# Ten products of zeros ahead of a row search, and transform steps issued three at a time, in a two-layer graph attention kernel

## What is computed

```python
xr = jnp.einsum('nd,rdf->rnf', x, W)              # one transform of all nodes per edge type
oi, oj = xr[etype, dst], xr[etype, src]
alpha = jax.nn.leaky_relu(oi @ q + oj @ k, 0.2)
m = segment_max(alpha, dst); e = exp(alpha - m[dst]); z = segment_sum(e, dst)
out = segment_sum((e / (z[dst] + 1e-16))[:, :, None] * oj, dst) + b
# h = elu(layer 1); out = layer 2 of h; result = layernorm(x + out)
```

## Time and profile before

| | |
|---|---|
| median of three executions | 1293.2 us (1292.36 to 1293.78) |
| the profiled execution's own time | 1294.57 us |
| its span, first to last instruction | 1292.6 us |
| PE busy | 1249.7 us, 97% of the span |
| DVE busy | 989.4 us, 77% |
| ACT busy | 757.7 us, 59% |
| mean granted clock of PE | 0.992 |

### The profile page before, as it was taken

How to read it: one execution, slowest core, us unless ns; L and a number is a source line. 1 busy time by engine, 2 the same in 40 slices (tenths; PEclk the granted TensorE clock), 3 DMA queues, 4 the chain that set the end, 5 groups by cost and what they waited for, 6 DMA issues and landing times.

```text
span 1292.6 us, 18743 instructions
## 1 busy us (share of the span) xinstructions
PE 1249.7 (97%) x7104; PEld 1121.7 (87%) x7104; DVE 989.4 (77%) x1289; ACT 757.7 (59%) x1210; POOL 4.9 (0%) x20
## 2 busy tenths in 40 slices
PE   6899999999999999999999999999989999999996
PEld 4766656665699999999999999999989999999995
DVE  4678899999399899999989967759844466656554
ACT  4655432332499889979979942257434444464462
POOL 1000000000000000000000000000000000000000
PEclk9999999999999999999999999999989999999998
DMA  9420131111553333323313237944486776778860
GB/s 314 164 92 31 44 122 49 50 50 43 194 122 103 103 96 103 96 68 116 118 50 99 64 109 236 313 160 159 159 307 235 248 246 204 264 261 305 283 230 34
DMA packets 93847, 195.32 MB, mean 151 GB/s; under 512 B 16125, under 2 KB 66366, under 8 KB 93762
## 3 DMA queue, kind: packets, MB, share of 16 engines
q1 hardware_dynamic: 93568, 193.77, 45.1%
q0 software_dynamic: 96, 0.23, 0.1%
q10 hardware_dynamic: 98, 0.16, 0.0%
HBM read 154.28 MB, written 39.85 MB: 150 GB/s over the span
## 4 chain that ended last, share of the span: by engine, by line
PE 76%; DVE 13%; ACT 4%; DMA 3%; issue 3%; SPq 1%; PEld 1%; ACTq 0%; DVEq 0%
PE ps L1174 24%; PE ps L1132 24%; PE ps L959 13%; PE ps L984 10%; DMA arena<-in_L_gnn_W 3%; DVE arena L1319 3%; PE ps L1036 3%; DVE arena L1376 2%; DVE arena L1380 2%; ACT arena L718 1%; ACT arena L719 1%; DVE ps L1448 1%; DVE misc L1329 1%; DVE arena L1461 1%; DVE arena L1398 1%
## 5 line engine op out<-in xcount | busy, mean ns | idle before, releaser
L1132 PE MATMUL ps<-arena 128*128 128x193 f32 x2400 | 396.9, 327 | 1.8 <-DVE arena L1380 1.5
L1132 PEld LDWEIGHTS ps<-arena 128*128 128x128 f32 x2400 | 392.1, 190 | 4.3 <-DVE arena L1380 3.8
L959 PE MATMUL ps<-arena,xT 128*128 128x384 f32 (+1 forms) x720 | 249.6, 494 | 0.0
L718 ACT ACTIVATE arena<-arena,misc 128x640 f32<-128x640 f32 x240 | 196.9, 820 | 31.5 <-DVE arena L1376 23.7
L959 PEld LDWEIGHTS ps<-arena,xT 128*128 128x128 f32 x720 | 131.4, 191 | 76.4 <-issue 0.3
L719 ACT ACTIVATE arena<-arena,misc 128x640 f32<-128x640 f32 x240 | 195.7, 815 | 0.0
L1376 DVE TENSOR_TENSOR arena<-arena 128x1280 f32<-128x1280 f32 x120 | 178.4, 1486 | 20.9 <-ACT arena L719 20.8
L1380 DVE SCALAR_TENSOR_TENSOR arena<-arena,Ct 128x1280 f32<-128x1280 f32 x120 | 179.2, 1493 | 15.0 <-DVE arena L1376 11.0
L1319 DVE SCALAR_TENSOR_TENSOR arena<-arena,misc 128x1250 f32<-128x1250 bf16 x108 | 155.8, 1520 | 1.5 <-ACT arena L663 1.5
L835 ACT ACTIVATE g_hi<-arena 128x512 fp32r<-128x512 f32 (+2 forms) x90 | 49.7, 552 | 158.8 <-PE ps L1174 143.6
L1174 PE MATMUL ps<-x2a,g_hi 128*128 128x384 f32 (+1 forms) x600 | 131.8, 342 | 5.2 <-issue 5.2
(11 more groups left out here) (174 smaller groups left out, 1356.8 us busy)
## 6 DMA issues: line engine op xcount, KB each, us to landing
x2a<-xr_d SPq DMA_DIRECT2D x45, 776.0 KB, 4.3
x2b<-xr_d SPq DMA_DIRECT2D x45, 776.0 KB, 4.5
arena<-xr_d SPq DMA_DIRECT2D x120, 193.0 KB, 2.4
xr_d<-stg SPq DMA_DIRECT2D x60, 384.0 KB, 3.0
arena<-ab_d SPq DMA_DIRECT2D x12, 1280.0 KB, 6.4
xr_d<-bb SPq DMA_DIRECT2D x60, 193.0 KB, 2.2
arena<-in_L_gnn_W SPq DMA_DIRECT2D x5, 2304.0 KB, 9.8
arena<-in_L_gnn_W SPq DMA_DIRECT2D x7, 1152.0 KB, 6.8
```

The costliest lines, as they stand in the source:

```text
L718: nc.scalar.activation(weights1(g, r, t)[:, h, :], abr[:, r, h, :], ACT.Exp, bias=qk1t[:, t, col + R * H:col + R * H + 1])
L959: last = mm(unit1_bank(u)[:, 0:w], xT[:, kt, t * P:(t + 1) * P], v, start=kt == 0, stop=kt == KT - 1)
L1132: last = mm(bank1(g, i)[:, o:o + HD + 1], weights1(g, r, t)[:, h, i * P:(i + 1) * P], xring[t % NX][:, o:o + HD + 1], start=False, stop=Tr ...
```

## The change

Two edits. First, PE issues NWARM = 10 products of zeros (bf16, 128 by 128 by 512 columns, into `ps[3]`, which nothing has written yet and whose next use starts afresh) after its wait for the constants and ahead of its wait for `ranks`. Second, `steps0` gives BATCH = 3 steps at a time: 20 batches over the same 79 pairs, so behind pairs 30, 34, 38 and so on to 102, and behind pair 105. No step is added or left out; the order among pairs and among steps stays. ACT's count of the units that are still to be taken out after the loop follows the new rule and is the same one unit.

```diff
         RUNS_AT = 4
+        NWARM = 10
+        BATCH = 3
         FLAG_AT = 1
 
         def steps0(pair):
 
             n = PAIRS - T_AT
-            return range(max(0, NK0 * (pair - T_AT) // n), max(0, NK0 * (pair + 1 - T_AT) // n))
+            done = [max(0, NK0 // BATCH * (p - T_AT) // n) * BATCH for p in (pair, pair + 1)]
+            return range(*done)
...
-            for u in range(NK0 * (PAIRS - 1 - T_AT) // (PAIRS - T_AT) // KT, NL):
+            for u in range(steps0(PAIRS - 1)[0] // KT, NL):
                 transform_out(u)
...
+            for i in range(NWARM):
+                mm(ps[3][:, :], zm[:, 0:P], zm[:, :], start=True, stop=True)
             pe.wait_ge(S["ranks"], 1)
```

## The result

Median 1313.62 us (1311.62 to 1314.01) against 1293.49 us before, run beside it; the ratio is 1.0153, 95% interval 1.0139 to 1.0167. The medians differ by 20.1 us, slower, where +20.0 was forecast. The profiled execution took 1313.7 us, its span is 1311.7 us, 19.1 more than before.

The account below looks back on a forecast made before the run. PE was taken to bound the kernel through the pair loop, so its delay there moves everything after. The loop's +20.2 us and the front's -0.2 gave +20.0 on 1293.2: 1313.2 us, eight-in-ten range 1308 to 1317.

Parts of the forecast that it names:

- The turn: Pair loop, four pairs and three steps: 4.50 us instead of 3.41, +1.09 each, over 18 turns.
- D: Fourth pair between two batches (A is the first): starts 2.10 us after A, waiting for DVE's quad.
- The rival with ACT alone: Pair loop: only ACT's copy gates, turn 3.86 us, +9.5 us, about 1302.5 us; chance 0.06.
- The rival in which all waits are hidden: Pair loop: batches only save changes of product, 1290.5 to 1292 us; chance 0.05.
- The rival with the clock: Pair loop: clock falls again and again, a half-clock turn 7.2 us, about 1337 us in all; chance 0.07.
- The start of the loop: Pairs 26 to 31: half clock kept, pair 31 at 74.5 us against 74.37 before, +0.1 us.
- The ten products: Zeros at the kernel's front: -0.2 us, bounds +0.3 to -1.9, since the W1 block lands at 33.1 us regardless.
- a sign that the front is a term of its own: Front: the first product at L913 behind the W1 block moving from 33.1 us would show the prediction wrong.
- The sum: Whole kernel: +20.2 us for PE's loop and -0.2 for the front, +20.0 on 1293.2, giving 1313.2 us.

Follow-up runs that it names:

- the run with odd pairs and the late unit: Changed kernel with batches behind pairs 31, 35, ... 103, and ACT taking a finished unit out behind its copy of the fourth pair after the batch: 1.0060, 1300.29 us.
- e2_batches_only: Changed kernel without the products of zeros (NWARM = 0), batches of three kept: ratio 1.0157 to the kernel before, 1313.48 us.

## Why the prediction was right

**The mechanism** was the one named. The turn was forecast at 4.50 us from four latencies of the trace before, and is 4.50; 18 of them at 81.0, measured 154.75 - 73.82 = 80.9. D was forecast 2.10 us behind A, measured 2.08. That DVE's wait binds and ACT's is covered by it is shown by the run with even pairs and four banks: with ACT's wait gone the time stays (1.0147, and 1.0153 with it). That it is the place of the batches in the quad, and not batching, is shown by the runs with odd pairs: 1.0103 with two banks, 0.9990 with four.

**The rival with ACT alone** is wrong for this kernel, but is what the run with odd pairs and the late unit does: forecast 3.86 us a turn, measured 3.89. **The rival in which all waits are hidden** is what four banks and odd pairs make of it; its gain was forecast at 1.2 us from 40 saved changes of product, and the medians give 0.6 and 1.1 us, both within the noise of the times. **The rival with the clock** didn't come: with PE busy 82% of the time the granted clock was 1.00 over 81 us. The Trainium skill ("TensorE: Matmul & The Clock Gate", "A second HAM failure mode: psum-queue depth-cycling") tells of a clock that swings when PE idles briefly and often between groups of products, without saying how long those idles were. No such swing shows here, with idles of 0.34 and 0.48 us in each turn of 4.50.

**The start of the loop** was off by 0.7 us: pair 31 was forecast at 74.5 us and came at 73.82. I had kept the half clock at 70.15 to 73.56, over the first steps. In this profile it lay from 68.3 to 71.6 us, some 2 us earlier, over pairs 26 to 30, which wait for ACT and DVE anyway. The batch began at 71.74 instead of 71.25, but its steps took 2.08 us at the full clock instead of 3.2.

**The ten products** were forecast at -0.2 us; the first pair came 0.24 us earlier, and alone they made 1.0001 in the time. That the 0.24 fits is luck: the first pair starts at 39.5 to 41.5 us in the eight profiles with zeros and at 39.45 to 41.1 in the three without. And one step of the working was wrong. I had the x transposes end 2 to 3 us early and the block of W1 gate as before. In fact the second part of x landed later, at 27.4 us, and the transposes ended at 33.9, behind the block. The prediction had named a first product behind that block that moves from 33.1 us as a sign that the front is a term of its own; it moved to 33.80, so that sign came, and what it is worth doesn't show in the time. The wait of 1.7 us behind which I kept the half clock vanished; the half clock lay behind the wait of 3.7 us instead, at 27.3 to 30.6 us:

```profile
26.00:32.00 6.00, 4.58 (x26) 4.37 (x26) 5.61 (x13) 2.81 (x6) 0.00 (x0) 0.72 1.02 389
```

**The sum** against the profile: +19.4 us at the hand-over, +19.1 in the span, where +20.0 was forecast; the medians differ by 20.1. With the front's 0.2 us taken off, pair 31 was forecast at 74.3, so the start of the loop makes 0.5 us of the difference in the trace. That forecast and medians agree to 0.1 us is luck, since single executions of one kernel differ by 2 us and more.

## What to carry to other kernels

Work that fills an engine between dependent steps must stand where the waits are: three fillers in a row cover one wait well and leave the next ones bare, and the price is the latency of the loop round the other engines, read from the trace as start-to-start times. With a double buffer that is refilled a group at a time, the place of a break within the group decides: one pair further on cost 7 us less, at no change in work. When two waits stand one behind the other, removing the smaller one gives nothing; it shows up again in the larger.

A faster start buys nothing where a transfer sets the pace: the rank products came down by 1.7 us, and the kernel's time by nothing that shows.

## What the runs showed that was not expected

The stretches of half clock don't lie at fixed places. Without the zeros PE ran at half clock at 32.6 to 36 us in one profile, and not at all there in another with the same instructions up to the loop, while the stretch near 70 us was twice as long (`e2_batches_only`; PE busy 4.44 of 6 us in the first row):

```profile
30.00:36.00 6.00, 4.44 (x41) 3.26 (x41) 5.68 (x13) 3.43 (x11) 0.00 (x0) 1.00 1.03 398
...
66.50:73.00 6.50, 6.25 (x29) 4.50 (x29) 2.93 (x4) 2.46 (x6) 0.00 (x0) 0.50 0.77 305
```

The same profile, PE in order of time:

```profile
32.46 1.53 PE L916 MATMUL ps<-ident,arena 128*128 128x128 f32 x12 [1.25 <-DMA arena<-in_L_gnn_W]
...
39.45 0.49 PE L1041 MATMUL ps<-arena 128*128 128x180 bf16 x4
```

The first pair came 1.5 us earlier there than in the kernel before (40.97). Of this 0.65 us are the block of W1, which landed earlier (32.46 against 33.11); from there to the first pair it took 6.99 us against 7.86. So some 0.9 us of the difference between two executions come from where a half-clock stretch falls. The granted clock in the profile reads 1.00 from the first microsecond, though the products of the first 15 us of the kernel before ran at half speed (0.225 us for a transpose that later takes 0.11): at the start the length of the products has to be read, not that column.
